# Attention and feed-forward on one core: the first pass runs 42 units ahead of the scores in place of 46

## What is computed

```python
qk = (x @ Wqk_w.T + Wqk_b)          # 8 heads x 8 values x (q, k)
v  = x @ Wv_w.T + Wv_b
scores = einsum('bhqd,bhkd->bhqk', q, k)
attn = softmax(scores, axis=-1) / sqrt(64)
out  = (attn @ v) @ Wo_w.T + Wo_b
x = layernorm(x + out)
Wg, Wu, Wd = dequant(int4 weights, scales by groups of 128)   # 512 -> 1792 -> 512
x = layernorm(x + (silu(x @ Wg.T) * (x @ Wu.T)) @ Wd.T)
```

## Time and profile before

| what | value |
|---|---|
| median of 3 runs | 521.27 us |
| the profiled execution, device time | 521.81 us |
| its span in the trace | 519.7 us |
| PE busy | 501.1 us, 96% |
| DVE busy | 413.0 us, 79% |
| ACT busy | 405.5 us, 78% |
| reductions of the first pass (L1249) | 256, 157.0 us |
| exponentials (L760) | 128, 140.5 us |
| first-pass products (L963) | 256, 60.8 us |
| granted clock of PE | 0.998 of full speed |

### The profile page before, as it was taken

The page is one execution under the profiler, slowest core; times in us unless marked ns, Lnnn a source line. Parts: engine busy times, 40 slices in busy tenths (PEclk is TensorE's granted clock), DMA queues, the critical chain, the costliest instruction groups (busy, mean ns, idle before and its releaser), DMA issues.

```text
span 519.7 us, 8086 instructions
## 1 busy us (share of the span) xinstructions
PE 501.1 (96%) x2976; PEld 193.2 (37%) x2976; DVE 413.0 (79%) x705; ACT 405.5 (78%) x558; POOL 255.7 (49%) x295
## 2 busy tenths in 40 slices
PE   8899999999999999999999999999999999999994
PEld 3222222323222322234444444444444444444441
DVE  3699999989999997368878778778668666788677
ACT  1522888998899989877888888888888888888880
POOL 9100091823100715073464676664997962648741
PEclk9999999999999999999999999999999999999999
DMA  6410018576530005700031121140020020000022
GB/s 192 136 68 5 21 35 211 182 144 125 91 59 1 3 5 103 276 7 1 1 59 24 20 43 21 20 62 1 1 81 1 0 83 0 3 0 1 0 81 81
DMA packets 30151, 29.20 MB, mean 56 GB/s; under 512 B 19489, under 2 KB 21921, under 8 KB 29857
## 3 DMA queue, kind: packets, MB, share of 16 engines
q1 hardware_dynamic: 26688, 22.67, 15.7%
q0 software_dynamic: 3424, 6.03, 6.3%
HBM read 24.37 MB, written 4.23 MB: 55 GB/s over the span
## 4 chain that ended last, share of the span: by engine, by line
PE 79%; DVE 7%; POOL 5%; ACT 5%; issue 2%; DMA 1%; SPq 0%; DVEq 0%; POOLq 0%; ACTq 0%
PE ps L1123 16%; PE ps L1135 16%; PE ps L1157 16%; PE ps L1068 9%; PE ps L1039 6%; PE ps L963 6%; DVE mxh L1249 4%; ACT pbuf L760 3%; PE ps L892 3%; POOL x L617 2%; PE ps L1051 1%; PE ps L902 1%; PE ps L1016 1%; POOL stack L663 1%; DMA arena<-xT 1%
## 5 line engine op out<-in xcount | busy, mean ns | idle before, releaser
L1249 DVE TENSOR_REDUCE mxh<-ps 128x1 f32<-128x512 f32 x256 | 157.0, 680 | 6.5 <-PE ps L963 5.3
L760 ACT ACTIVATE pbuf<-ps,gamma 128x1024 f32<-128x1024 f32 x128 | 140.5, 1114 | 16.2 <-PE ps L1039 11.2
L841 ACT ACTIVATE ps<-ps,ratio 128x512 f32<-128x512 f32 x168 | 106.5, 659 | 40.4 <-PE ps L1123 37.3
L1157 PE MATMUL ps<-wd,stack 128*128 128x512 f16 x440 | 129.7, 379 | 0.7 <-POOL stack L663 0.6
L1123 PE MATMUL ps<-arena,wg 128*128 128x512 f16 x448 | 115.5, 379 | 0.1
L1135 PE MATMUL ps<-arena,wu 128*128 128x512 f16 x448 | 115.3, 379 | 0.1
L1423 DVE TENSOR_TENSOR ps<-ps,stack 128x512 f32<-128x512 f32 x128 | 87.8, 695 | 33.4 <-PE ps L1157 31.7
L847 ACT ACTIVATE ps<-ps,ratio 128x512 f32<-128x512 f32 x156 | 98.9, 659 | 6.6 <-PE ps L1135 2.3
L661 POOL CAST stack<-pbuf 128x512 f16<-128x512 f32 x55 | 33.5, 609 | 76.5 <-DVE pbuf L1398 76.5
L1423 DVE TENSOR_TENSOR ps<-ps,pbuf 128x512 f32<-128x512 f32 x76 | 52.6, 695 | 23.2 <-PE ps L1157 22.5
L1068 PE MATMUL ps<-pbuf,arena 128*32 128x256 f32 x832 | 66.5, 391 | 1.7 <-ACT avt L767 1.7
(11 more groups left out here) (120 smaller groups left out, 387.4 us busy)
## 6 DMA issues: line engine op xcount, KB each, us to landing
arena<-xT SPq DMA_DIRECT2D x16, 256.0 KB, 5.8
x<-x SPq DMA_DIRECT2D x2, 2048.0 KB, 10.0
out<-x SPq DMA_DIRECT2D x3, 1024.0 KB, 4.2
stack<-down_ratios SPq DMA_DIRECT2D x1, 2048.0 KB, 9.6
wg<-gq POOLq DMA_DIRECT2D x4, 448.0 KB, 7.3
wu<-uq POOLq DMA_DIRECT2D x4, 448.0 KB, 7.4
wd<-dq POOLq DMA_DIRECT2D x2, 896.0 KB, 10.3
pbuf<-down_ratios SPq DMA_DIRECT2D x1, 1536.0 KB, 6.2
```

What stands on the lines that cost most here:

```text
L760: nc.scalar.activation(pbuf[:, pi % 4, :].rearrange("p (a n) -> p a n", a=2), ps[:, at:at + 2, :], ACT.Exp, scale=gamma[:, n // (ALL // B) ...
L841: nc.scalar.activation(gbank[t % 2], gbank[t % 2], ACT.Copy, scale=gr[:, t % G, c:c + 1])\
L1157: mm = nc.tensor.matmul(bank[k], mparts[:, a, t % NM, k * P:(k + 1) * P], wd[:, i, :], start=(i == 0 and a == 0), stop=(a == 1), skip_grou ...
L1249: nc.vector.tensor_reduce(mxh[:, f % 2, qh, half:half + 1], ring_bank("first", n), AX.X, ALU.max)\
```

## The change

AHEAD becomes 42, so every unit after the opening is issued one step later. The turn of a group's maxima moves from step 8f - 3 to 8f - 2. In the first step of a group (not step 0) the two units of pair 0 come ahead of the scores. The drain begins at step 54, and its side tasks move with it. In the opening, the pieces keep their order, but those from key 17 on get earlier keys, and three pieces follow the one before after a single unit.

```diff
-AHEAD = FG + 14
+AHEAD = FG + 10
...
-            f, r = divmod(n + 3, KT)
+            f, r = divmod(n + 2, KT)
...
-        DRAIN = ALL - 11
+        DRAIN = ALL - 10
...
-                     13: [(put, 7)], 15: [second[1]], 17: [second[2]], 19: [(put, 8)], 21: [second[3]], 23: [second[4]],
...
+                     13: [(put, 7)], 15: [second[1]], 16: [second[2]], 18: [(put, 8)], 20: [second[3]], 21: [second[4]],
...
                 for pair in range(2):
+                    new_group = n and n % KT == 0 and pair == 0
+                    if new_group:
+                        for use in ring_uses_at(n, pair):
+                            ring_use(*use)
                     scores(n, pair)
-                    for use in ring_uses_at(n, pair):
-                        ring_use(*use)
+                    if not new_group:
+                        for use in ring_uses_at(n, pair):
+                            ring_use(*use)
```

More of the change, by code:

```diff
@@ L1090, in _ @@
             later = {1: [(put, 3)], 3: [turn_v], 5: [(put, 4)], 7: [(put, 5)], 9: [(put, 6)], 11: [second[0]],
-                     13: [(put, 7)], 15: [second[1]], 17: [second[2]], 19: [(put, 8)], 21: [second[3]], 23: [second[4]],
-                     25: [(put, 9)], 27: [second[5]], 29: [second[6]], 31: [(put, 10)], 33: [second[7]], 35: [second[9]],
-                     37: [(put, 11)], 40: [second[10]], 42: [second[8]], 44: [second[11]], 46: [second[12]]}
+                     13: [(put, 7)], 15: [second[1]], 16: [second[2]], 18: [(put, 8)], 20: [second[3]], 21: [second[4]],
+                     23: [(put, 9)], 25: [second[5]], 26: [second[6]], 28: [(put, 10)], 30: [second[7]], 32: [second[9]],
+                     34: [(put, 11)], 36: [second[10]], 38: [second[8]], 40: [second[11]], 42: [second[12]]}
             for n, use in enumerate(before):
```

## The result

The changed kernel took **523.36 us** (median of 8 runs, 522.74 to 524.13) against 521.42 (521.0 to 522.84, 8 runs) of the kernel before beside it: a ratio of 1.0030 with a 95% interval of 1.0017 to 1.0042. It is slower by 0.17 to 0.42%, that is by 0.9 to 2.2 us. The prediction was 523.1 us.

A forecast was written before the change was run, and what follows sets the result against it. PE was taken to pace the opening, DVE the steady steps and ACT the end of attention. The terms -0.6 + 2.4 - 2.05 + 2.1 = +1.85 us, added to the 521.27 us median, gave 523.1 us; range 520.6 to 525.2.

The forecast's parts named there:

- The opening, -0.6: Four units fewer before attention save 0.6 us, between 0 if PE sets the pace and 2.4 if DVE does.
- One more step with units and six boundaries, 2.4 + 2.1: Before the drain: one more step with first-pass work, +2.4 us; six group starts at 0.35 us each, +2.1 us.
- T + 3.75: At a group's start: the maxima transfer lets PE start the scores 3.75 us after the turn of the maxima starts.
- The estimate from the Trainium skill: Landing of the maxima transfer by the skill's 2.0 us fixed cost: 0.1 us later than the rows give.
- the 0.07 of the first step: In a group's first step DVE's queue ends before the early units are ready: 0.07 us idle.
- One drain step less, -2.05: At the end of attention the last step, two exponentials without a side task, falls away: -2.05 us.
- The seventh boundary, 0: The group start inside the drain costs 0, at most 0.5 us, as one exponential is queued while scores wait.
- the last reduction: Sign in the changed profile: DVE's last reduction comes some 3.9 us later than in the kernel before.
- the feed-forward part: Sign in the changed profile: the part behind attention, untouched by the change, starts about 2 us later.
- Rival B: DVE's three banks and the early units hide the boundaries: -0.25 us, 521.0 us; chance 0.17.
- rival C: Boundaries hidden and opening DVE-paced, so all four reductions leave it: -2.05 us, 519.2 us; chance 0.12.
- Rival D: Maxima transfer takes 2.92 us or lands behind the load of x, drain waits 0.5: +4.0, 525.3 us; chance 0.09.

The follow-up runs named there:

- The packed 46: Kernel before with the opening's 23 pieces at the changed kernel's packed keys, 46 units still ahead: 524.21 us, ratio 1.0039.
- after: The changed kernel of this study, with the whole change, against the kernel before: 523.36 us, ratio 1.0030.
- the kernel without the gap: Kernel before with packed opening and 46 units ahead, but the last three pieces spread again: 523.16 us, ratio 1.0026.

## Why the prediction was right

**The opening, -0.6.** -0.66. Near the PE-paced end of its two ends, for the reason given: a lone unit costs PE what a pair costs. The packed 46 confirm it from the other side.

**One more step with units and six boundaries, 2.4 + 2.1.** 4.71 us between the first exponential and the last combining: 2.39 for the step leaves 2.32, or 0.385 for each boundary on average, where 0.35 was worked out. By the distances it is 0.33 to 0.42 in five groups and 0.60 in the third, whose output turns the prediction left out. By hand the scores stood at T + 3.73 and were released at T + 3.75; they came at T + 3.77, with 2.67 us from the issue to the scores (154.44 to 157.11), where the prediction took 2.65. The run without the new order shows the landing more directly, since PE there waits for nothing else: T = 154.12, scores at 157.91, T + 3.79, and T + 3.78 to 3.88 over its six boundaries. So my rows were 0.03 to 0.13 too early. The estimate from the Trainium skill, "DMA: Bandwidth & Descriptors", "Anatomy of one DMA", was T + 3.85, inside what was measured. That section gives its 2.0 us for transfers that GpSimd issues, and these are issued by SP, so the agreement is no test of it. DVE idles 0.38 behind the sum's copy, 0.35 was forecast; the 0.07 of the first step shows as 0.11 of small gaps.

**Whose price it is.** The prediction called the boundary's price the remains of the wait for the transfer, with the early units as a part remedy. The mechanism was right in its timing but incomplete in its cause. The units ahead of the scores cost 0.33 a boundary even with the maxima landed long before (the new order alone), and 0.32 with the turn half a step earlier (20.69 against 20.37). The late turn without them costs 0.45 to 0.5 (the change without the new order, and the late turn alone). Each edit delays the group's first scores by 0.4 to 0.6 us, and they share one price: they don't add up.

**One drain step less, -2.05.** -2.56. The step removed is worth what was said: the last stretch has 26.15 us with the side tasks moved and 24.14 in after, 2.01 less. The term was mis-sized by 0.5, because the side tasks that move with DRAIN were costed at nothing, and the move makes the last 14 exponentials 0.57 us shorter (15.04 to 14.47). The kernel with that move alone has it: -0.55, where the turn of the seventh sum no longer makes PE wait 0.71 us. The prediction looked only at whether the last task's results come in time, not at what the tasks did to ACT on the way.

**The seventh boundary, 0.** Right in after, and only there: in the kernel with the late turn alone it costs 1.15 us.

The sum by the trace is -0.66 + 4.71 - 2.56 = +1.49 us against +1.85 forecast, and the medians differ by 1.94. That the medians lie within 0.1 of the forecast is partly luck: their difference is known to 0.9 to 2.2 us only, and by the traces two terms missed in opposite directions, the middle by +0.2 and the drain by -0.5. Of the signs named beforehand, the last reduction is 4.05 us later counted from the first unit (3.9 was said), and the feed-forward part starts 1.49 us later (2 was said). Rival B (20.4 us between the issues) and rival C (an opening ending near 49 us) are refuted by the rows at 20.70 and 49.95; that first scores row has 0.60 us of earlier start in it. Rival D wanted a distance above 20.9 and is not there: the distances without output turns are 20.70 to 20.78.

## What to carry to other kernels

In this kernel two engines are both full and hand work on through three banks. There a wait wasn't hidden by putting other work in front of it, since this work itself needs the full engine: the delay moved one step on and cost nearly the same. Cutting prefetched work pays only if it relieves the engine that sets the pace; here four reductions fewer freed DVE in a stretch that PE paced. And of a move of side tasks, read the whole row of the pacing engine before and after, not only whether the last of them is in time. When a small transfer is issued earlier, look at what else the DMA engines carry at that moment: half a step earlier, one of them came while they were full, and the scores came 4.14 us behind its issue instead of 2.67 to 2.78.

## What was not expected of the hardware

**TensorE's clock fell to 1.2 GHz** (0.50 granted) in 55 to 60 us of the kernel with the packed opening and 46 units, right after the stretch in which PE was left with single matmuls waiting for banks. With the projections put back into this stretch it stayed at 1.00. The busy time ahead doesn't tell them apart: PE was busy 4.18 of 5.00 us around the start of the fall, while the kernel with the output turns apart kept its clock behind 4.06 us:

```profile
50.00:55.00 5.00, 4.06 (x25) 0.96 (x24) 4.66 (x10) 4.46 (x5) 0.00 (x0) 1.00 0.25 62
```

Nor does the number of matmuls clearly: 17 in that stretch, where the kernel of this row has 25 and the one without the gap 19. The Trainium skill, "TensorE: Matmul & The Clock Gate", Part 1, has the clock go down after idle time; here no idle time ahead of the fall was over 0.40 us. What exactly made it fall is left open.

Its price shows best inside the five runs of that kernel, which differ in their mean granted clock: 524.24 and 524.99 us at 0.990, 524.0 and 524.21 at 0.995, and 523.0 at 0.996. The last is the time of the kernel without the gap (523.16), which had 0.996 to 0.999. So where the clock fell it cost some 1 to 2 us, an estimate from these few runs, and it did not fall as far in each run. In the profiled executions of all the other kernels the clock was at 1.00 from 45 to 70 us.

**A lone first-pass matmul costs TensorE as much time as a pair** on two halves of its rows: 0.32 us to the next instruction (34.41 to 34.73) and 0.32 (31.87 to 32.19).

**Executions differ in their start.** The first unit came between 20.6 and 21.8 us, by when the first loads landed (the chain ahead of it waits for the transfers of xT, 4.32 us in after and 5.54 in before), with nothing changed in the kernel there. Two single traces can't be compared by their spans to better than that; counted from the first unit they can.
